# A vision tower on one core: the patches tokenized in two halves, the layer norm's offset sums moved to TensorE, and the first half's attention issued ahead of the second half's tokens

## What is computed

```python
tokens = tokens.reshape(B, h * wgrid, p * p * C5)        # five shifted copies of the image, 16x16 patches
mean = jnp.mean(tokens, axis=-1, keepdims=True)
var = jnp.var(tokens, axis=-1, keepdims=True)
normed = (tokens - mean) * jax.lax.rsqrt(var + LN_EPS) * ln_gamma + ln_beta
h = jnp.einsum('bnd,de->bne', normed, w) + b             # 16 tokens of 192 per image
...
qkv = (x @ w_qkv + b_qkv).reshape(b, n, 3, h, d)         # x is the layer norm of h, 12 heads of 16
attn = jnp.einsum('bihd,bjhd->bhij', q, k) * scale       # the diagonal masked out but for token 0
out = jnp.einsum('bhij,bjhd->bihd', softmax(attn), v)
h = h + out @ w_proj + b_proj
```

## Time and profile before

| | |
|---|---|
| median of 3 runs | 756.3 us (755.73 to 757.66) |
| the profiled execution, its own time | 755.92 us |
| its span in the trace | 754.1 us |
| PE busy | 674.5 us (89%) |
| DVE busy | 417.2 us (55%) |
| POOL busy | 328.3 us (44%) |
| ACT busy | 237.0 us (31%) |
| PE on the chain that ended last | 70% |
| DVE on it | 17% |

### The profile page before, as it was taken

How to read it: one execution, slowest core, us unless ns; L and a number is a source line. 1 busy time by engine, 2 the same in 40 slices (tenths; PEclk the granted TensorE clock), 3 DMA queues, 4 the chain that set the end, 5 groups by cost and what they waited for, 6 DMA issues and landing times.

```text
span 754.1 us, 20181 instructions
## 1 busy us (share of the span) xinstructions
PE 674.5 (89%) x6420; PEld 571.7 (76%) x6420; DVE 417.2 (55%) x1246; ACT 237.0 (31%) x675; POOL 328.3 (44%) x296
## 2 busy tenths in 40 slices
PE   6957858888989999857699899999999999999995
PEld 5724645656665688744599799999999999999994
DVE  6874574665378868878733344444444444444442
ACT  3112312112327511213343233333333333333331
POOL 4830630021022554410445456555555455655654
PEclk9967968668999999985599999999999999999998
DMA  8910000000000000232237655565445566465422
GB/s 342 251 36 3 3 3 1 3 2 3 1 0 1 1 2 21 107 111 97 44 105 219 176 130 129 140 170 115 114 124 176 146 172 173 115 172 124 100 46 39
DMA packets 34983, 70.05 MB, mean 93 GB/s; under 512 B 6353, under 2 KB 21234, under 8 KB 34930
## 3 DMA queue, kind: packets, MB, share of 16 engines
q0 software_dynamic: 15840, 17.71, 13.8%
q10 hardware_dynamic: 8064, 33.12, 12.8%
q1 hardware_dynamic: 11026, 18.48, 8.0%
HBM read 59.31 MB, written 9.98 MB: 92 GB/s over the span
## 4 chain that ended last, share of the span: by engine, by line
PE 70%; DVE 17%; DMA 6%; issue 4%; POOL 1%; ACT 1%; POOLq 0%; DVEq 0%; SPq 0%; ACTq 0%
PE bank L1575 18%; PE bank L1567 13%; PE bank L1570 8%; PE bank L1329 4%; DMA out_dram<-arena,number_u 4%; PE bank L1397 4%; PE bank L1547 3%; PE bank L1274 3%; PE bank L1349 3%; DVE stats L916 1%; DVE zx L930 1%; PE bank L1367 1%; PE bank L1340 1%; DVE arena L1150 1%; DVE arena L1147 1%
## 5 line engine op out<-in xcount | busy, mean ns | idle before, releaser
L653 POOL DMA_INDIRECT out_dram<-arena,number_u x80 | 126.7, 1584 | 50.2 <-DMA out_dram<-arena,number_u 22.7
L647 POOL DMA_INDIRECT arena<-normed_rows,fetch_u x80 | 78.4, 980 | 113.9 <-DMA out_dram<-arena,number_u 45.7
L826 ACT ACTIVATE arena<-bank,arena 128x128 f32<-128x128 f32 x234 | 64.7, 375 | 116.1 <-PE bank L1570 116.1
L1234 DVE COPY arena<-bank 128x256 f32<-128x256 f32 x81 | 34.4, 425 | 118.9 <-PE bank L1547 106.4
L1575 PE MATMUL bank<-arena 128*128 128x192 f32 x468 | 82.9, 326 | 0.0
L1575 PEld LDWEIGHTS bank<-arena 128*128 128x128 f32 x468 | 75.3, 190 | 0.2 <-ACT arena L826 0.2
L1253 DVE TENSOR_SCALAR arena<-bank,arena 128x192 f32 x80 | 33.4, 418 | 58.7 <-PE bank L1575 56.1
L550 POOL TENSOR_SCALAR rstd<-mv 128x4 f32<-128x4 f32 (+1 forms) x15 | 3.4, 227 | 140.8 <-DVE mv L919 140.8
L1567 PE MATMUL bank<-arena 128*128 128x128 f32 x468 | 59.0, 276 | 2.9 <-DVE arena L1234 2.8
L1567 PEld LDWEIGHTS bank<-arena 128*128 128x128 f32 x468 | 57.0, 192 | 4.1 <-DVE arena L1234 3.8
L826 ACT ACTIVATE arena<-bank,w_space 128x128 f32<-128x128 f32 x132 | 36.4, 375 | 68.3 <-PE bank L1570 68.3
(11 more groups left out here) (253 smaller groups left out, 1262.4 us busy)
## 6 DMA issues: line engine op xcount, KB each, us to landing
arena<-in_moe_w_dram ACTq DMA_DIRECT2D x14, 579.0 KB, 5.9
arena<-in_moe_w_dram ACTq DMA_DIRECT2D x14, 576.0 KB, 4.4
arena<-in_xf_dram SPq DMA_DIRECT2D x8, 512.0 KB, 10.2
w_space<-in_moe_w_dram ACTq DMA_DIRECT2D x7, 579.0 KB, 5.3
w2small<-in_moe_w_dram ACTq DMA_DIRECT2D x7, 579.0 KB, 5.5
w_space<-in_moe_w_dram ACTq DMA_DIRECT2D x7, 576.0 KB, 4.2
wab<-in_moe_w_dram ACTq DMA_DIRECT2D x7, 576.0 KB, 3.8
arena<-in_w_dram SPq DMA_DIRECT2D x8, 480.0 KB, 9.6
```

The lines of the kernel that those rows point to most:

```text
L647: pool.indirect_dma_start(out=mo_stage[:, s * ROWN:(s + 1) * ROWN], out_offset=None, in_=normed_rows, in_offset=bass.IndirectOffsetOnAxis( ...
L653: pool.indirect_dma_start(out=out, out_offset=bass.IndirectOffsetOnAxis(ap=number_u[:, s:s + 1], axis=0), in_=mo_res[:, s * D:(s + 1) * D] ...
L826: nc.scalar.activation(mo_hT[:, m, :], bank[2 + m][:, 0:P], ACT.Gelu, bias=b1[:, m:m + 1]).then_inc(free[2 + m], 1)
L1234: nc.vector.tensor_copy(mo_xT.rearrange("p k t -> p (k t)"), bank[1][:, 0:2 * P]).then_inc(free[1], 1)
```

## The change

The order list changes up to the layer norm that follows the first attention (`("ln", "z", 0)`) and not behind it. Seven things change.

- Pixels are loaded in halves: filters and 256 KB of first-half pixels chunk by chunk, then `tokb`, then the eight second halves, then the constants.
- PE sums four of the five shifts of the offset (`betas`, column groups of its array, bank 4), from a widened copy of the offsets that ACT makes; ACT stores the sums, and PE adds them with a product by ones. DVE keeps the fifth shift (`beta_part(c)`), and takes `foldsum` over from POOL (`fold_part(c)`).
- The squares are made, summed and stored by half (`SQUARES`, banks 5 and 7).
- PE tokenizes tiles 0 to 3 first. The eight chunks of tiles 4 to 7 are new entries `pixels`: six ahead of the first half's `xT`, two behind it.
- The tokens of the second half on DVE (`("tok", "T", 1)`), its layer norm and transposes come behind the first half's scores, and its `qk` between the `av` entries of the first half.
- `V` of the first half comes ahead of `bias`, and `V` of the second half behind the first `av`.
- POOL clears one half's value tiles at each `xT`, right behind the inverse root of that half's layer norm.

```diff
     return [
-        ("tok", "T", 0), ("ln", "A", 0), ("put", "A", 0), ("tok", "T", 1), ("ln", "A", 1), ("xT", "A", 0), ("put", "A", 1), ("qk", "A", (0, 0)),
-        ("qk", "A", (0, 1)), ("xT", "A", 1), ("front", "A", (0, 0)), ("front", "A", (0, 1)), ("back", "A", (0, 0)), ("qk", "A", (1, 0)),
-        ("back", "A", (0, 1)), ("bias", "A", 0), ("V", "A", 0), ("av", "A", (0, 0)), ("V", "A", 1), ("gumbel", "B", 0), ("av", "A", (0, 1)),
-        ("av", "A", (0, 2)), ("av", "A", (0, 3)), ("av", "A", (0, 4)), ("qk", "A", (1, 1)), ("av", "A", (0, 5)), ("ln", "z", 0),
+        ("tok", "T", 0), ("pixels", "T", (0, 6)), ("ln", "A", 0), ("put", "A", 0), ("xT", "A", 0), ("pixels", "T", (6, 8)), ("qk", "A", (0, 0)),
+        ("qk", "A", (0, 1)), ("front", "A", (0, 0)), ("front", "A", (0, 1)), ("back", "A", (0, 0)), ("tok", "T", 1), ("V", "A", 0), ("bias", "A", 0),
+        ("back", "A", (0, 1)), ("ln", "A", 1), ("av", "A", (0, 0)), ("put", "A", 1), ("av", "A", (0, 1)), ("xT", "A", 1), ("V", "A", 1),
+        ("gumbel", "B", 0), ("av", "A", (0, 2)), ("qk", "A", (1, 0)), ("av", "A", (0, 3)), ("av", "A", (0, 4)), ("qk", "A", (1, 1)), ("av", "A", (0, 5)), ("ln", "z", 0),
...
-                sp.dma_start(xf[:, c], a["xf"][c]).then_inc(sem(f"in_pixels{c}"), 16)
+                sp.dma_start(xf[0][:, c], a["xf"][c, :, 0:HALF]).then_inc(sem(f"in_pixels{c}"), 16)
             load(sp, "tokb", tokb[:], a["tokb"])
+            for c in range(FC):
+                sp.dma_start(xf[1][:, c], a["xf"][c, :, HALF:TOK]).then_inc(sem(f"in_later{c}"), 16)
...
+                elif step_name == "xT" and L == "A":
+                    clear_values(n)
...
+            loaded(act, "fold")
+            nc.scalar.activation(beta_wide.rearrange("p v c m -> p (v c) m"), repeat(fold[:, NSH * FC:(NSH + ONPE) * FC], 2, SQ), ACT.Copy).then_inc(sem("beta_widened"), 1)
+            square(0, 0, FC)
+            square(1, 0, FC // 2)
+            act.wait_ge(sem("beta_sums"), 1)
+            nc.scalar.activation(beta_rows, bank[BETAS][:, 0:D], ACT.Copy, scale=1.0 / SQ).then_inc(sem("beta_rows"), 1)
+            store_squares(0)
+            square(1, FC // 2, FC)
...
-                if step_name == "xT":
+                if step_name == "tok" and n == 1:
+                    store_squares(1)
+                elif step_name == "xT":
...
-                    if c:
-                        beta_part(c - 1, v)
+                    if c and v == 0:
+                        fold_part(c - 1)
+                    if c and v == 2:
+                        beta_part(c - 1)
...
+                for c in range(FC):
+                    betas(c)
+                    squares(0, c)
+                    tokens(0, c)
                 loaded(pe, "tokb")
+                mm(bank[0][:, 256:256 + D], ones[0:1, :], tokb[:], start=False, stop=False, skip_group_check=True)
+                pe.wait_ge(sem("beta_step"), FC)
                 mm(bank[0][:, 256:256 + D], ones[0:FP, :], betasum, start=False, stop=False, skip_group_check=True)
+                pe.wait_ge(sem("fold_step"), FC)
                 mm(bank[1][:, 256:256 + D], ones[0:FP, :], foldsum, start=False, stop=True, skip_group_check=True)
+                pe.wait_ge(sem("beta_rows"), 1)
+                mm(bank[0][:, 256:256 + D], ones[:], beta_rows, start=False, stop=True, skip_group_check=True)
+                square_columns(0)
+
+            def later_pixels(c0, c1):
+                for c in range(c0, c1):
+                    tokens(1, c)
+                    squares(1, c)
...
+                elif step_name == "pixels":
+                    later_pixels(*n)
+                elif step_name == "tok":
+                    square_columns(1)
```

More of the change, by code:

```diff
@@ L501, in _, with widen_count @@
             tt = nc.gpsimd.tensor_tensor
-            def fold_sums():
+            def widen_count():
                 loaded(pool, "fold")
                 nc.gpsimd.tensor_copy(cnt_wide[:], repeat(cnt, 2, SQ)).then_inc(sem("cnt_widened"), 1)
[L508 to L513, removed]
             def tok_rstd(n):
@@ L1265, in _, with tokens, squares @@
             pe.wait_ge(sem("ones_set"), 2)
+            def tokens(n, c):
+                pe.wait_ge(sem("weff"), c + 1)
+                pe.wait_ge(sem(f"in_later{c}" if n else f"in_pixels{c}"), 16)
+                for t in range(*GROUPS[n]):
+                    ps = claim("tok", t) if c == 0 else bank[t]
+                    at = (t - 4 * n) * P
+                    mm(ps[:, 0:D + 1], xf[n][:, c, at:at + P], weff[:, c, :], start=(c == 0), stop=(c == FC - 1))
+            def squares(n, c):
+                pe.wait_ge(sem("squares"), squared[n, c])
+                for q in range(4):
+                    ins = mm(bank[SQUARES[n]][q * SQ:(q + 1) * SQ, SQUARES_AT:SQUARES_AT + P], cnt_wide[:, c, :], xsq[n][:, c, q * P:(q + 1) * P],
+                             start=(n == 0 and c == 0), stop=(c == FC - 1), skip_group_check=True)
+                if c == FC - 1:
+                    ins.then_inc(sem("square_sums"), 1)
@@ new lines, in _, with betas, square_columns @@
+            squared = {(0, c): c + 1 for c in range(FC)} | {(1, c): FC + c + 1 for c in range(FC)}
+            def betas(c):
+                pe.wait_ge(sem(f"in_filters{c}"), 16)
+                for v in range(ONPE):
+                    ins = mm(bank[BETAS][v * SQ:(v + 1) * SQ, 0:D], beta_wide[:, v, c, :], w5[:, c, v, :], start=(c == 0), stop=(c == FC - 1), skip_group_check=True)
+                if c == FC - 1:
+                    ins.then_inc(sem("beta_sums"), 1)
+            def square_columns(n):
+                pe.wait_ge(sem("square_rows"), n + 1)
+                for t in range(*GROUPS[n]):
+                    q = (t - 4 * n) * SQ
+                    mm(bank[t][:, D + 1:D + 2], square_rows[q:q + 1, n * P:(n + 1) * P], ones[q:q + 1, 0:1], start=False, stop=True, skip_group_check=True).then_inc(full_of("tok", t), 1)
@@ L1283, in square_columns @@
-                def square_columns(t0, t1):
-                    for t in range(t0, t1):
-                        q, at = t // 2 * SQ, t % 2 * P
-                        mm(bank[t][:, D + 1:D + 2], square_rows[q:q + 1, at:at + P], ones[q:q + 1, 0:1], start=False, stop=True, skip_group_check=True).then_inc(full_of("tok", t), 1)
-                pe.wait_ge(sem("cnt_widened"), 1)
-                for c in range(FC - 1):
-                    pe.wait_ge(sem("weff"), c + 1)
-                    pe.wait_ge(sem(f"in_pixels{c}"), 16)
-                    tokens(c, 0, T)
-                    squares(c)
@@ L1305, in tokenize @@
-                square_columns(0, T // 2)
-                tokens(c, T // 2, T)
-                square_columns(T // 2, T)
-                loaded(pe, "const")
+                pe.wait_ge(sem("beta_rows"), 1)
+                mm(bank[0][:, 256:256 + D], ones[:], beta_rows, start=False, stop=True, skip_group_check=True)
+                square_columns(0)
+            def later_pixels(c0, c1):
+                for c in range(c0, c1):
+                    tokens(1, c)
+                    squares(1, c)
+                if c1 == FC:
+                    loaded(pe, "const")
```

72 lines of the change are left out of this document (34 added, 38 removed).

## The result

The changed kernel takes 767.5 us (median of 4 runs, 765.9 to 769.1) where the kernel before took 757.0 beside it: a ratio of 1.0126, interval 1.0086 to 1.0165. Timed a second time with the experiments it took 766.3 against 757.8, ratio 1.0128 (1.0087 to 1.0169). By these ratios it is slower by about 9.5 us (the medians differ by 10.5 and 8.5). Forecast were 760.9, 5.0 us slower, and a range up to 764.0: the sign was right, the size half of what came.

A forecast was written before the change was run, and what follows sets the result against it. The prediction took the chain through PE and DVE up to the second half's scores as the bound: an earlier head, then exposed second-half work, put those scores 5.0 us later. 755.92 + 5.0 = 760.9 us, range 752.3 to 764.

The forecast's parts named there:

- What the list exposes: Second half's tokens, statistics and normed tiles move behind the first half's softmax; second half's scores at 102.5, 5.0 us later.
- The head: Tokenization up to DVE's first token read: 2.45 us a chunk, read at 29.7 behind the constants, 7.1 us earlier.
- Sixteen products of values at the low clock: Values of each half on PE, priced at 4.88 us at 1.2 GHz.
- The bias product: PE's multiplication behind the first half's values, priced at 0.85 us; DVE held 1.5 us for the bias.
- The normed tiles of the second half: DVE's tiles behind the second inverse root: 1.25 us, after a hold of 1.1 or 0 by POOL's fill.
- Whatever this start shifts by, the end shifts by: Behind the second half's scores nothing is reordered, so their 5.0 us shift was added to the profiled 755.92 us.
- the late constants: Rival at DVE's first token read: constants land at 32.0, all behind slips 2.3 us, 763.2 us; chance 0.07.
- the case on the other side: Rival: PE's clock stays up through the first half's scores and waits, saving 6.6 us, 754.3 us; chance 0.20.
- The lock: Rival: DVE wins the shared ports from POOL's fills, both holds (1.35 and 1.1 us) vanish, 758.5 us; chance 0.13.

The follow-up runs named there:

- e1: The new tokenization with the order list of the kernel before, all eight later chunks behind the first half's; 755.5 us, ratio 0.9944.
- the table of twelve: Stations, median times and ratios of the twelve follow-up kernels, each timed beside the kernel before; the changed kernel's repeat is one of them.
- the first execution: The changed kernel's first profiled execution, from the first comparison; 769.08 us.
- e2: The changed kernel with the four constants loaded ahead of the second halves of the pixels; 762.8 us, ratio 1.0052.
- the second execution: The profiled execution of the changed kernel when it was timed again unchanged as a control; 766.28 us.
- e13: e8 with four products of the identity with itself in TensorE's wait ahead of the first half's queries; 753.1 us, ratio 0.9933.
- the repeat: The changed kernel timed a second time, unchanged, as a control beside the experiments; 766.3 us, ratio 1.0128.
- e6: The changed kernel with the last two pixel chunks moved from ahead of the first half's queries to behind its second score; 763.2 us, ratio 1.0085.
- e7: The changed kernel with ten products of the identity with itself in each of three TensorE waits; 763.8 us, ratio 1.0077.
- e12: The changed kernel with the second half's token reading and statistics moved back ahead of the first half's queries; 763.9 us, ratio 1.0080.
- e10: e1 with all five shifts of the offset sums on VectorE again, none on TensorE and ScalarE; 763.1 us, ratio 1.0080.
- e4: The changed kernel with GpSimd's value-tile fills and iota cast moved away from VectorE's normed tiles; 762.7 us, ratio 1.0045.
- e8: e1 with constants ahead of the second half's pixels, and GpSimd's clearing and cast moved off VectorE's normed tiles; 752.0 us, ratio 0.9933.

## Why the prediction was right in sign and half in size

*What the list exposes* was the right mechanism: e1 takes the list back and is 11 us faster. In the table of twelve, second half's scores at 90 to 95 go with 752 to 758 us and those at 100 to 105 with 763 to 766 (within the upper band the times don't follow them), and no such order shows by the first half's. The step that failed is the size of that mechanism: the sum has the second half's scores 5.0 us later, and they came 10.8 and 7.8 us later. Three terms of the sum were too small, in the first execution the constants were late as well, and what the forecast adds the shift to was a short execution.

*The head* held, in part by luck. A chunk on DVE took 2.39 (2.45 forecast). The first read came at 29.31 to 30.04 in six profiles with the constants where the change put them (29.7 forecast) and at 31.21 and 31.47 in two, always with the constants ending the wait; with them issued earlier (e2) the columns ended it. But the forecast kept the old issue at 17.62 and the old 12.1 us to landing; the last constant was issued at 20.50 and 20.90 and landed after 11.0 and 8.6. The two errors nearly cancel in the second execution. The first execution had a late one, 1.8 us, and then a second loss: PE waited 1.93 us ahead of its transposes, the granted clock was 0.58 over 44 to 48, and the two chunks took 5.2 us (43.57 to 48.76) instead of 3.9. In the second execution that wait was 0.75, the clock 1.00, the chunks 3.6. These two terms make the first profile later than the second; in the second the first half's values start at 66.27, 0.5 ahead of the forecast, and the end is still 5.4 late.

*Three terms behind that were too small*, and the second execution gives them without the others. Sixteen products of values at the low clock took 5.49 and 5.46, not the 4.88 of the earlier trace rows, 0.6 each: over those 4.88 us of the kernel before the granted clock was 0.57, so they were not wholly at the lower level; here it was 0.50. The bias product was priced by a projection at the high clock (0.85) although the values ahead of it were priced at the low one; it took 1.62, and DVE was held for 2.76 us instead of 1.5. The normed tiles of the second half were priced with the fill alone (1.1); but the cast of the indices and POOL's additions to `h` stand behind that fill. The fill held DVE for 0.95 us, the cast for 0.7 and two additions for 0.5, and DVE's four tiles took 3.45 instead of 2.35. Together 0.6 + 0.8 + 1.1 + 0.6 = 3.1 us, which takes -0.5 at the first values to +2.7 at the scores.

*"Whatever this start shifts by, the end shifts by"* was taken to the last microsecond, from one execution, and a single execution can't carry that. From DVE's take-up of the second half's first score to the end the kernel before needed 755.92 - 101.8 = 654.1 us, the least of all fourteen profiled executions; the changed kernel 656.8 and 657.0, the others up to 662.7 (e13). In the repeat the next 230 us took 231.6 instead of 230.1, the rest 425.4 instead of 424.0; in e13 233.3 and 429.5. So of the 5.4 us by which the repeat's end missed the forecast, 2.7 were there at the scores and 2.6 came behind them. But the kernel before itself ran from 753.2 to 763.1 beside the experiments, with medians of 757.8 to 758.5: the 755.92 that the shift was added to lies some 2 us under them. Between the medians the end shifted by 10.5 and 8.5 us where the scores shifted by 10.8 and 7.8, so that the rule fails on the mean is not shown. Nor do e6, e7 and e12 show it: their scores came 3.7 to 5.0 us earlier than the repeat's, their times 2.4 to 3.1 by the medians and 3.3 to 3.9 by the ratios, with intervals as wide as the difference. What stretches these untouched stages by up to 8.6 us was not tried and stays open. A part lies in PE's own work: over the whole stretch PE is busy 602.1 us in e13 and 596.9 in the kernel before.

*The rivals.* The clock did not stay up (0.50 over 62 to 94), so the case on the other side fell, but its price was real: e7 shows 2.97 us for the values, where it had 2.70. The lock went POOL's way each time. The high end of the range lay at 764, since it took the late constants as the only thing beyond the sum; the scatter of the 650 us behind has no term in it.

What I never asked is what the new tokenization does without the list. The 5.3 us of what e10 keeps and the 7.6 us of the sums nearly cancel, and the working had both inside one term, the earlier first read.

## What to carry to other kernels

When a list is reordered so that one half starts earlier, look up which idle time of the other engine the displaced work had been filling: here 9.1 us of VectorE's busy time had lain beside TensorE's queries, and no early score paid for it. Take a change apart into its independent moves before judging it: the parts here pulled in opposite directions, and the new tokenization with its sums on TensorE (7.6 us) could be kept without the list that cost 11 (e1). And measure how much the untouched rest varies between executions before adding a shift to it to the last microsecond, or reading a gain of 2 us off the stations of one profile.

## What the runs showed of the hardware

VectorE's normed tiles were held by GpSimd's instructions, one after the other. Four of them take 1.25 us alone, 2.27 with one fill of 1.37 beside them, 1.79 in e4 beside additions to `h`, 3.46 in the changed kernel beside a fill, the cast and two additions (82.95 to 86.41), and 4.31 in e1 beside both fills and the cast:

```profile
52.27 2.70 POOL L557 MEMSET arena<- 128x1536 f32 x2
52.35 4.31 DVE L956 TENSOR_SCALAR zx<-h,mv,rstd 128x192 f32<-128x192 f32 x4 [1.47 <-POOL rstd L552]
...
54.91 1.05 POOL L596 CAST iota_wide<-iota 128x1024 f16<-128x1024 f32 x1
```

In the changed kernel's first execution the four tiles end at 84.27, 85.27, 85.84 and 86.41, each about 0.1 us behind one GpSimd instruction (the fill ends at 84.16, the cast at 85.16, two additions at 85.72 and 86.29). In e1 the first tile was held through both fills (52.35 to 55.07; the second fill ends at 54.96) and the second tile through the cast (it ends at 56.08, the cast at 55.96). So a waiting tile got through behind the last fill and behind the cast, and not between the two fills; what makes the difference is not shown. The Trainium skill, *SBUF — State Buffer*, section "Who interferes with whom", has the one that issues first hold the shared ports for its whole instruction where a VectorE instruction runs in a 2-port mode; the runs agree with the blocking, and no run here shows the mode.

TensorE's granted clock fell behind some waits of a microsecond or two, and not behind others like them. In the changed kernel a wait of 1.93 us ahead of the transposes was followed by 0.58 over 44 to 48 us in the first execution, and one of 0.75 by 1.00 in the second. With waits of 0.58 and 0.93 ahead of the queries e8's clock was 0.82, 0.50 and 0.83 in the windows 46 to 48, 48 to 50 and 50 to 52 us; with waits of 0.57 and 0.93 in the same places e1's was 1.00 over all its queries (45.86 to 52.94), and with four products in the second wait e13's was 1.00 in all three windows. What decides is not shown.
